# A fused eight-layer gated model on one core: tiles of the first half issued at once in both expert mixtures, the second half's routing in eight pieces between the first nine tiles

## What is computed

```python
def _L0_ffn_ref(x, router_w, w1, w2):
    probs = jax.nn.softmax(xf @ router_w.T, axis=-1)
    topv, topi = jax.lax.top_k(probs, 2)
    topv = topv / (topv.sum(axis=-1, keepdims=True) + 1e-09)
    h = jax.nn.gelu(jnp.einsum('td,edh->teh', xf, w1), approximate=False)
    y = jnp.einsum('teh,ehd->ted', h, w2)
    out = jnp.einsum('te,ted->td', cw, y)
def _L3_ffn_ref(x, Wg, Ws1, Ws3, Ws2, We1, We3, We2):
    gates = jax.nn.sigmoid(xf @ Wg)
    vals, idx = jax.lax.top_k(gates, TOP_K)
    vals = vals / vals.sum(axis=-1, keepdims=True)
    shared = jax.nn.silu(xf @ Ws1) * (xf @ Ws3) @ Ws2
    h = jax.nn.silu(jnp.einsum('td,edf->tef', xf, We1)) * jnp.einsum('td,edf->tef', xf, We3)
    out = (shared + routed) / (N_SHARED + TOP_K)
```

## Time and profile before

| | |
|---|---|
| median of three runs | 1840.54 us |
| time of the profiled execution | 1836.82 us |
| its span, first to last instruction | 1835.1 us |
| mean granted TensorE clock | 0.917 of full |
| busy share of the span | PE 83%, PEld 65%, DVE 59%, ACT 37%, POOL 43% |
| layer 0's mixture in the span | from about 304 us to about 555 us |
| layer 3's mixture in the span | from about 1602 us to the end |

### The profile page before, as it was taken

How to read it: one execution, slowest core, us unless ns; L and a number is a source line. 1 busy time by engine, 2 the same in 40 slices (tenths; PEclk the granted TensorE clock), 3 DMA queues, 4 the chain that set the end, 5 groups by cost and what they waited for, 6 DMA issues and landing times. The chain is left out here.

```text
span 1835.1 us, 32265 instructions
## 1 busy us (share of the span) xinstructions
PE 1515.9 (83%) x10543; PEld 1188.7 (65%) x10543; DVE 1082.8 (59%) x2434; ACT 683.5 (37%) x1673; POOL 782.4 (43%) x1037
## 2 busy tenths in 40 slices
PE   2998786799905786888887888789999999869997
PEld 1776675699904654666664444578778788658874
DVE  2666763323436978677775888455465765444555
ACT  2555443233304332344443333244454544411121
POOL 1444374513362444344443333145445377533335
PEclk9999897899955588899998999899999999969999
DMA  8000003477610000000000000000000000048853
GB/s 276 28 0 2 1 26 108 142 224 234 191 51 4 0 1 1 1 0 0 0 0 1 0 0 0 1 1 0 0 1 1 1 17 15 25 126 238 234 160 87
DMA packets 90876, 100.94 MB, mean 55 GB/s; under 512 B 11156, under 2 KB 73804, under 8 KB 90125
## 3 DMA queue, kind: packets, MB, share of 16 engines
q1 hardware_dynamic: 53490, 69.07, 12.2%
q0 software_dynamic: 8192, 16.79, 3.2%
q10 hardware_dynamic: 29083, 13.66, 2.6%
HBM read 70.92 MB, written 28.57 MB: 54 GB/s over the span
## 5 line engine op out<-in xcount | busy, mean ns | idle before, releaser
L427 POOL TENSOR_TENSOR exp_scores<-exp_scores,softmax_recip 128x308 f32<-128x308 f32 x256 | 181.7, 742 | 242.8 <-DVE softmax_recip L590 242.7
L916 POOL DMA_INDIRECT gathered_rows_ffn<-sorted_y,slot_ffn x128 | 121.0, 945 | 212.5 <-DMA sorted_y<-expert_rows_ffn 143.0
L612 PE MATMUL psum<-identity,exp_scores 128*77 128x128 f32 x1024 | 157.0, 290 | 41.1 <-POOL exp_scores L427 37.9
L1115 PE MATMUL psum<-sorted_transposed_ffn,tile_weights_ffn 128*128 128x256 f32 x736 | 184.2, 394 | 2.5 <-DVE sorted_transposed_ffn L1023 2.4
L612 PEld LDWEIGHTS psum<-identity,exp_scores 128*77 128x77 f32 x1024 | 119.6, 154 | 66.6 <-issue 32.6
L1773 POOL TENSOR_TENSOR exp_scores_xattn<-exp_scores_xattn,softmax_recip_xattn 128x1640 f32<-128x1640 f32 x32 | 93.5, 2921 | 160.8 <-DVE softmax_recip_xattn L1946 160.8
L442 ACT COPY probs_transposed<-psum 77x512 f32<-77x512 f32 x192 | 111.8, 584 | 131.8 <-PE psum L612 130.3
L1115 PEld LDWEIGHTS psum<-sorted_transposed_ffn,tile_weights_ffn 128*128 128x128 f32 x736 | 135.8, 195 | 27.6 <-DVE sorted_transposed_ffn L1023 12.2
L1124 PE MATMUL psum<-tile_weights_ffn,hidden_ffn 128*128 128x128 f32 x1104 | 138.5, 276 | 0.0
L700 PE MATMUL psum<-probs_transposed,v_padded 77*32 77x128 f32 x2048 | 128.9, 275 | 6.7 <-ACT probs_transposed L442 6.7
L1124 PEld LDWEIGHTS psum<-tile_weights_ffn,hidden_ffn 128*128 128x128 f32 x1104 | 131.0, 192 | 0.2
(11 more groups left out here) (358 smaller groups left out, 3402.8 us busy)
## 6 DMA issues: line engine op xcount, KB each, us to landing
tile_weights_ffn<-in_L_ffn_packed_dram SPq DMA_DIRECT2D x46, 512.0 KB, 3.5
tile_weights_ffn<-in_L_ffn_packed_dram SPq DMA_DIRECT2D x46, 384.0 KB, 3.4
sorted_rows_ffn<-sorted_x SPq DMA_DIRECT2D x92, 128.0 KB, 3.9
sorted_y<-expert_rows_ffn ACTq DMA_DIRECT2D x92, 128.0 KB, 3.3
sorted_x<-zeros SPq DMA_DIRECT2D x4, 1472.0 KB, 13.7
x_residual<-in_x_dram SPq DMA_DIRECT2D x4, 512.0 KB, 11.6
sorted_x<-xn_ffn,slot_ffn POOLq DMA_INDIRECT x128, 2.2
gathered_rows_ffn<-sorted_y,slot_ffn POOLq DMA_INDIRECT x128, 3.0
```

The lines of the kernel that those rows point to most:

```text
L427: nc.gpsimd.tensor_tensor(e[:, par, heads, :], e[:, par, heads, :], rec.to_broadcast([S, HG, KC]), ALU.mult).then_inc(s["probs_ready"], 1)
L612: last = nc.tensor.transpose(m.psum[0:KC, 4 + g % 2, h * S:(h + 1) * S], e[:, nxt, g * HG + h, :], m.ident[:, :])
L916: nc.gpsimd.indirect_dma_start(yg[:, n % 4, k, :], None, m.sorted_y[half][:, :], bass.IndirectOffsetOnAxis(slot[:, half, k, b:b + 1], 0)). ...
L1115: mm = nc.tensor.matmul(m.psum[:, 2 * (n % 2) + half, c * TILE:(c + 1) * TILE], w[:, n % DEPTH, at:at + 128], xst[:, n % 2, :], start=True ...
```

## The change

In both mixtures PE no longer has the second half's routing and the wait for `ranked` ahead of tile 0. The routing's work on each engine is cut into pieces that stand between the tiles. The four groups of four transposes (`group`) and their router products (`logits`) stand within the first three tiles, DVE's chain is `route_last(n)`, called behind the y copy of tile n for n = 2 to 8, and the exponent stands on ACT behind tile 3's activation. The 32 scatters of the second half wait for `ranked` as before, which is now signalled behind tile 7's y copy. The PSUM regions of the routing move to the upper half of bank 7 and to banks 4 and 5, which adds some waits on PE (`xts_ready`, `y_ready`, `exp_wanted`, `counts_read`). The parts of the diff below are from the names, DVE, ACT and PE, in this order.

```diff
@@
+        LAST = HALVES - 1
+        WANT, PICK, COUNT = 2, 3, 6
...
+                def route_last(n):
+                    if n == WANT:
+                        dve.wait_ge(s["logits_in_psum"], PGROUPS)
...
+                            nc.vector.tensor_copy(p, raw).then_inc(s["exp_wanted"], 1)
+                    if n == PICK:
+                        dve.wait_ge(s["exp_ready"], 1)
+                        pick_first(nc, m, r, LAST, link)
+                    if n == PICK + 1:
+                        pick_second(nc, m, r, LAST, link, s["picked"])
+                    if n == PICK + 2:
+                        weigh_experts(nc, m, r, LAST, link)
+                    if n == COUNT:
+                        dve.wait_ge(s["counted"], 1)
...
+                        rank_pairs(nc, m, r, link)
+                    if n == COUNT + 1:
+                        slots_of_pairs(nc, m, r, LAST, link, s["ranked"])
+                    if n == COUNT + 2:
+                        expert_of_tiles(nc, m, r, LAST, link, s["tiles_known"])
...
                 transposed(0)
+                rstd_of_x(nc, m, dve, s["sd_ready"], s["rstd_ready"], s["shift_ready"])
+                normalise(0)
+                normalise(1)
                 if layer == 3:
                     gated(0)
                 transposed(1)
+                normalise(2)
+                normalise(3)
@@
+                    if n == 0:
+                        copy_group(0)
+                        copy_group(1)
+                    if n in (1, 2):
+                        copy_group(n + 1)
+                    if n == PICK:
+                        act.wait_ge(s["exp_wanted"], 1)
+                        nc.scalar.activation(probs[:, LAST, :, :], probs[:, LAST, :, :], ACT.Exp,
+                                             scale=1.0 if layer == 0 else -1.0).then_inc(s["exp_ready"], 1)
@@
-                count_picks(HALVES - 1)
-                pe.wait_ge(s["ranked"], HALVES - PLACED)
...
                 transposes(1)
+                group(0)
+                group(1)
                 for n in range(NTILES):
                     if n + 1 < NTILES:
                         up(n + 1)
+                    if n == 1:
+                        logits(2)
+                    if n == WANT + 1:
+                        pe.wait_ge(s["exp_wanted"], 1)
+                    if n == COUNT + 1:
+                        pe.wait_ge(s["counts_read"], 2)
                     if n + 2 < NTILES:
                         transposes(n + 2)
+                    if n == 0:
+                        logits(0)
+                        logits(1)
+                    if n == WANT:
+                        logits(3)
+                    if n == COUNT:
+                        count_picks()
+                    if n < 2:
+                        group(2 + n)
+                        pe.wait_ge(s["xts_ready"], 1 + 2 * n)
+                    if n == 2:
+                        pe.wait_ge(s["xts_ready"], 4)
                     down(n)
```

More of the change, by code:

```diff
@@ L762, in pick_experts, with pick_one, spread, pick_second @@
         link(nc.vector.reciprocal(p, p))
[L763 to L771, removed]
+    pick_one(nc, m, r, half, 0, link)
+def pick_one(nc, m, r, half, k, link):
+    p, wide, pk = r.probs[:, half, :, :], [S, HBATCH, E0], r.pick[:, k, :, :]
+    def spread(t):
+        return t.unsqueeze(2).to_broadcast(wide)
+    down = m.down[:, 0:E0].unsqueeze(1).to_broadcast(wide)
+    link(nc.vector.tensor_reduce(r.top[:, k, :], p, AX.X, ALU.max))
+    link(nc.vector.tensor_tensor(pk, p, spread(r.top[:, k, :]), ALU.is_ge))
+    link(nc.vector.tensor_tensor(pk, pk, down, ALU.mult))
+    link(nc.vector.tensor_reduce(r.work[:, :], pk, AX.X, ALU.max))
+    link(nc.vector.tensor_tensor(pk, pk, spread(r.work[:, :]), ALU.is_equal))
+    if k == 0:
+        link(nc.vector.scalar_tensor_tensor(p, pk, -4.0, p, ALU.mult, ALU.add))
+def pick_second(nc, m, r, half, link, picked):
+    pick_one(nc, m, r, half, 1, link)
     nc.vector.tensor_tensor(r.either[:, half, :].rearrange("p (b e) -> p b e", e=E0), r.pick[:, 0, :, :], r.pick[:, 1, :, :], ALU.add).then_inc(picked, 1)
+def pick_experts(nc, m, r, half, link, picked):
+    pick_first(nc, m, r, half, link)
+    pick_second(nc, m, r, half, link, picked)
 def weigh_experts(nc, m, r, half, link):
@@ L922, in _, with copy_group @@
                 nc.scalar.activation(m.sd[:, :], m.var[:, :], ACT.Sqrt, bias=m.eps[:, 0:1]).then_inc(s["sd_ready"], 1)
[L923 to L938, removed]
+                def copy_group(g):
+                    act.wait_ge(s["xt_in_psum"], g + 1)
+                    if g >= 2 and not shared:
+                        act.wait_ge(s["logits_in_psum"], g - 1)
+                    at = FIRST_GROUP + g if shared else g % 2
+                    nc.scalar.copy(xts[:, at * GT:(at + 1) * GT], m.psum[:, 4 + (g if g < 2 else 3 - g), :]).then_inc(s["xts_ready"], 1)
                 preload(nc, m, ACT.Gelu if layer == 0 else ACT.Silu)
@@ L1048, in _ @@
                         combine((done - 1) * HBATCH + at)
+                    route_last(n)
                 if shared:
@@ L1074, in _, with group @@
             def _(pe):
[L1075 to L1084 removed]
+                def group(g):
+                    pe.wait_ge(s["xn_ready"], g + 1)
+                    if g == 2:
+                        pe.wait_ge(s["xts_ready"], 2)
+                    if g == 3:
+                        pe.wait_ge(s["xts_ready"], 1)
+                        pe.wait_ge(s["y_ready"], 1)
```

87 lines of the change are left out of this document (35 added, 52 removed).

## The result

The changed kernel takes 1814.8 us, the median of four runs (1812.7 to 1815.3), beside 1840.5 for the kernel before (four runs). The ratio of the two is 0.9858, with a 95% interval of 0.9841 to 0.9875: 25.7 us faster, where 23.4 were forecast. The profiled execution took 1815.3 us, its span is 1813.5 us.

The account below looks back on a forecast made before the run. PE was taken to idle 22 to 23 us per mixture block on routing before tile 0, then bound the tiles, with a DVE ring in layer 3. Gains of 16.8 and 6.6 made 23.4: 1840.5 to 1817.1 us, range 1809 to 1828.

Parts of the forecast that it names:

- the early start: Tile 0 no longer waits for routing: layer 0's `down(0)` 19.8 us earlier, layer 3's `up(2)` 21.0 earlier.
- PE's later work: Router groups, transposes and counts that PE now does among later tiles: 2.4 us in each of layers 0 and 3.
- DVE's pieces: Routing pieces between tiles cost what exceeds DVE's slack: 0.6 us in layer 0; 4.4 in layer 3, exponent included.
- exponent: On ACT, between tiles: its table load delays layer 3's `gated(4)` by 1.1 us and costs layer 0 nothing.
- stand at the 24th tile: In layer 3 PE waits 5.4 us for tile 23's rows, behind the scatters; layer 0 just fits, 2.5 to spare.
- half clock behind it: After layer 3's stand PE restarts at half clock: 2.2 us lost, between bounds of 0 and 4.2.
- then the rows of tile 23 3.9: Layer 3's stand sum: 3.9 us for tile 23's rows after the last scatter lands, within 47.7 in all.
- rival B: Slow clock: half clock lasts 10.8 us after each start, losing 2.4 more each and 2.0 at the stand: 1824; chance 0.15.
- A: No stall in layer 3, so the 7.6 us of stall and clock stay gained: 1809.5; chance 0.12.
- C: New PE waits (`xts_ready`, `exp_wanted`, `counts_read`) land late, or layer 0 stands too: 6 to 10 more, 1823 to 1827; chance 0.12.
- D: Slower than before: scatters issue slower than one per 1.26 us; at 1.8 us an issue, 1849; chance 0.03.
- E: Nothing happens, as tile 0 is not in fact ready early; chance 0.03.

Follow-up runs that it names:

- store_first: The changed kernel with ACT issuing the store of tile 1 ahead of the exponent instead of behind it: 1810.9 us, one run.
- early_and_store: The changed kernel with the counts one tile earlier and the store of tile 1 ahead of the exponent: 1808.8 us, 0.9805 of the kernel before.
- count_late: The changed kernel with the counts, and so the scatters, two tiles later: 1823.2 us, 0.9895 of the kernel before.
- count_early: The changed kernel with the counts one tile earlier and the weighing of the experts last: 1810.3 us, 0.9823 of the kernel before.
- third set: Changed kernel, layer 3 alone, kernel before and a DVE-padded kernel, run on a slower chip; changed 1895.9 or 1894.4 us, padded 1894.6.

## Why the prediction was right, point by point

The time, 1814.8, lies 2.3 below the forecast of 1817.1, and on the first kind of chip every mechanism of the sum was found: the early start, PE's later work, DVE's pieces, one stand in layer 3 and none in layer 0. Some of the sizes were off, and that the total came so close is in part luck: the mixtures gave 27.6 us where 23.4 were counted, and 2 of the 4 us between them do not show in the medians.

**Layer 0** gained 17.1 (forecast 16.8), from two errors that cancel, which is luck. The start came 21.3 earlier, not 19.8: half a microsecond of it because tile 0 could be transposed sooner after the block's start, the rest mostly because PE was at full clock for both groups of transposes, which took 0.9 us (319.52 to 320.40) where 1.55 was counted. The later PE work was 2.35 (2.4). But "that is 0.25 + 0.35, say 0.6" for DVE's pieces was 1.8: the ranking cost 0.37 as counted, the first pick 1.42. The step that failed is the sentence on the exponent, "`down(4)` comes over 3 us after it: nothing". That held for Gelu and `down(4)`, but the store queued behind the exponent's wait was left out. store_first shows that it was worth 1.2.

**Layer 3** gained 10.5 (forecast 6.6). Term by term, from the starts of the `up`s and their distance from 3.11:

| term | forecast | measured |
|---|---|---|
| `up(2)` earlier | 21.0 | 23.2 |
| later PE work | 2.4 | 1.6 |
| exponent | 1.1 | 1.3 |
| first pick | 1.6 | 1.9 |
| half clock behind the first pick | none | 1.5 |
| second pick | 0.3 | 0 |
| ranking | 1.4 | 1.4 |
| stand at the 24th tile | 5.4 | 3.6 |
| half clock behind it | 2.2 | 1.5 |

These leave 10.4. The largest error is the stand with the half clock behind it, 5.1 in place of 7.6, and in the stand it is one number: "then the rows of tile 23 3.9". PE had them 2.1 us after their issue (1681.63 to 1683.72). The 3.9 is a median over 92 transfers, nearly all issued behind a tile's weights; this one had no weights right in front of it, as the next were issued at 1682.76. That this is why it was short is argued and not shown: in early_and_store the same transfer, in the same place, took 3.3. The second error is the start, 2.2. Tile 0 could be transposed 5.5 us after the block's start, where 6.8 was counted (its rows were used 3.1 us after their issue, 1593.95 to 1597.02, where 4.3 was taken from layer 0), and `up(2)` came 11.4 us behind that in place of 12.2. The clock rose 6 us after PE's restart, not after 10.8. So rival B had it wrong, and the choice of layer 0's clock as the model for both starts was right.

The half clock behind the first pick is the one thing in layer 3 that no term held. It was 1.5 us. It is absent in store_first and early_and_store, where the wait ahead of `up(6)` is 1.35 us, but also in count_late, where it is 1.66; in count_early, with 1.87, it is there. So it is no fixed cost of the changed kernel.

The rivals: A (no stand) did not happen, yet a third of its gain came, 2.5 of 7.6 us, since the stand and the slow clock behind it were shorter. C did not happen at the waits it names; its kind of loss came, in small, at a seam that it does not name, the store's 1.2 us in layer 0. D is excluded by the scatters' pace of 1.26 to 1.28, E by tile 0's releaser. Of the signs listed for being wrong, a stand in layer 0 too or none in layer 3, neither came up in the changed kernel's first trace. On the slower chips there was no stand in layer 3, so the account of the stand holds for the first kind of chip alone.

**The table load and the clock.** Between tiles the function behind the load starts 1.30 us after the load's start (337.60 to 338.90), and the exponent cost layer 3 1.3 us, the length of one load. The Trainium skill, "ScalarE: Activation LUTs", section "What ACT_TABLE_LOAD costs", adds a drain of about 1.38 us to every change of set; the trace shows none.

Behind the stand of 3.46 us the clock was 0.67, and with 0.44 of stand in count_early it stayed up. The Trainium skill, "TensorE: Matmul & The Clock Gate", section "HAM oscillation — how this bites in real kernels", says that a wait for data can make the next work start cold; the trace agrees, by the 0.67.

**The untouched blocks.** The 4.8 us that layer 0's attention lost in the first comparison go with the clock granted in that block, in every trace. The stretch from 150 to 200 us of the kernel before on the two slower chips, where attention ended at 312.5 and at 309.6:

```profile
150.00:200.00 50.00, 44.12 (x422) 36.88 (x421) 31.63 (x69) 25.47 (x52) 16.70 (x31) 0.86 0.01 2
...
150.00:200.00 50.00, 44.08 (x459) 36.49 (x457) 34.94 (x75) 26.82 (x57) 19.47 (x35) 0.97 0.01 2
```

So the same kernel has both. On chips like the first, attention ended at 304.5 (before) and 304.8 (count_late) with 0.97 in that stretch, and at 308.6 to 310.2 in the four others with 0.86 to 0.90. On the slower ones it ended at 309.3 and 309.6 with 0.97, and at 311.1 to 313.8 with 0.86 to 0.90. The lower grant needs no change of the kernel, then, and the new code does not force it. Of the nine traces with the new code in layer 0, eight have it, and of the five without, two; whether the change makes it more frequent is open, and so is its cause.

## What to carry to other kernels

When serial work is moved into a pipelined loop, its cost is the part of each piece that exceeds the slack behind it, so price the pieces one by one; but list too what each moved instruction has queued behind it, transfers above all. What the serial start used to cover gets a due time of its own: here 32 scatters, needed by the 24th tile. Shorten the chain to their release first, and let work that it does not need (the weights of the experts) go last: one tile earlier gave 4.5 us in layer 3. What is saved ahead of the release brings the tiles and the scatters forward alike and does not lengthen the stand: it stayed at 3.49 in store_first. For a landing time, look at single transfers in the same place and not only at the median of the group, and expect a spread: here 2.0 to 3.3 us in five traces, beside a median of 3.9.

## What the runs showed of the hardware

On the two slower chips the same kernels take 4.4% longer, and most of the difference, 76 of 85 us in the traces of the kernel before, sits in the mixtures: 289 and 275 us in place of 255 and 232. In their traces PE, ACT, DVE and SP all stop for 5 to 25 us while POOL issues its scatters at the usual pace. Transfers by queue in such a stretch of the changed kernel, third set, from 1700 to 1710 us, and in the first trace from 1660 to 1670 (packets, MB, share of 16 engines):

```profile
q0 software_dynamic: 265, 0.56, 16.6%
q1 hardware_dynamic: 309, 0.21, 6.4%
q10 hardware_dynamic: 272, 0.13, 4.5%
```

```profile
q1 hardware_dynamic: 1365, 1.66, 60.2%
q10 hardware_dynamic: 1054, 0.51, 17.1%
q0 software_dynamic: 276, 0.57, 14.7%
```

The scatters' own queue (q0) moves the same, the others nearly nothing. What the engines wait for is not named by the profile: of ACT's Silu in that stretch it says "remote", of PE's products "issue". The two queues of the kind "instruction" (q8 and q14) moved one packet each from 1684 to 1725 us there, and two each from 1643 to 1683 in the first trace, so no larger traffic on them is seen; what it is instead stays open. It nearly cancels in the comparison of two kernels on one chip, but it hid the stand that two of the sets were to measure.

The clock: a stand of PE of 0.44 or 1.53 us at the 24th tile was followed by products at full clock, one of 2.66, 3.46, 3.49 or 9.46 by products at half. At the first pick in layer 3, a wait of 1.94 or 1.87 behind one of 1.38 was followed by half clock, and one of 1.66 behind one of 1.38, or of 1.35 behind one of 1.24, was not; on the slower chips a wait of 1.90 to 1.95 at that place was followed by an `up` of 1.99 us, at full clock. So the length of one wait does not decide it alone.
